# A fused attention and mixture-of-experts kernel on one core: the second group's layer norm is computed ahead of the first unit's products

## Chip, cores and metric

The kernel runs on one core of one Trainium2 chip. The time is that of one execution on the device, in microseconds; three runs of the kernel before are shown. Engines are named as in the profile: PE is TensorE, DVE is VectorE, ACT is ScalarE, POOL is GpSimd, SP is SyncE, whose queue issues most loads and stores.

## What is computed

The input x has 16 batches of 128 channels by 256 positions. There are two stages, each gated and added to x:

```python
# stage 1: k = v = ctx, q = layernorm(x over the 256 positions), 16 heads of 8 channels
kv  = einsum('bhil,bhjl->bijhl', k, v)              # 8 x 8 products of a head
y   = causal convolution of kv with ssm_kernel      # one filter of 256 taps per head
out = einsum('bijhl,bhil->bjhl', y + kv * D, q)
x   = x + tanh(g_xattn) * out
# stage 2: xt = layernorm(x), 2048 tokens of width 256
probs = softmax(xt @ Wg); expert = argmax(probs)     # 8 experts, at most 256 tokens each
routed = gate * (silu(xt @ W1[e]) * (xt @ W3[e])) @ W2[e]
shared = (silu(xt @ sw1) * (xt @ sw3)) @ sw2
x   = x + tanh(g_ffn) * (routed + shared)
```

The layer norm subtracts the mean and divides by the root of the variance plus 1e-5. All arrays are float32.

## The kernel before

**Tiling of stage 1.** The 16 batches are cut into 4 groups of 4. A group's 16 heads are cut into 8 units of 2 heads, so stage 1 has 32 units, 0 to 31, and a unit has one slot of the main loop on each engine (`for s in range(SLOTS)`). The convolution of a head is a product with a Toeplitz matrix (tile `toep`), which the DMA engines read from a padded filter in memory.

- POOL and ACT multiply the context by itself into planes (tile `kv`, a ring of 5 sets of four heads): POOL the mixed products (`kv_products`, lines 433 and 436), ACT the squares (`squares`, line 697). A set serves two units. A set waits for its group's context and for a free place in the ring, that is, for sums of earlier units.
- PE convolves a unit (`convolve`, lines 1055 and 1058) into one of two PSUM tiles `z`. It needs the planes, the Toeplitz rows, and the products of the unit two before, which free its tile.
- DVE multiplies the sums by the queries (`products`, six instructions of line 452) and writes `terms`. It needs `z` and the group's queries `qr`.
- After the 8 units of a group, PE turns the terms back and sums them (`turn_r`, line 1083), and DVE adds them to x (`first_residual`, line 846).

**Queries of a group.** They come out of four steps on four engines. DVE takes the statistics (`norm_stats`, lines 822 to 828: four bn_stats, four bn_aggr, then the variance plus epsilon in `veps` and minus the mean in `mneg`). POOL takes the root by a power and the bias (`scale_and_bias`, lines 578 and 579). ACT applies both (`norm1`, line 676, four batches). PE turns the result (`turn_q`, line 1070), and ACT copies it out of PSUM (`q_copy`, lines 706 and 711). The second group's queries are read first by the products of unit 8.

**What sets the order.** Each engine runs its own list in program order, and semaphores join the lists. Two tables of slots, `STEPS` and `LAST_STEPS`, say at which slot of the loop a step of a group stands; `due(step, s)` gives the group whose step is due at slot s. For the second group (group 1) the statistics stand at slot 1, behind the products of unit 1; the root and the norm at slot 2, behind the planes of that slot; the turning at slot 5. Group 0 is prepared ahead of the loop. The semaphores `stats_done`, `rstd_done` and `xn_done` count the norms in the order of the list `norms`. `norm_stats` also waits until the root before has read `veps` and `mneg`, and `scale_and_bias` until the norm before has been applied.

**Around the first units.** Ahead of the loop DVE adds the skip weight to the diagonal of the first two Toeplitz matrices (line 990). In slot 4, behind the products of unit 4, it copies the router's weights into the shared weight tile (line 1004). POOL makes three constants (lines 594 to 598) between the third set of planes and the loop. The SP queue loads, in this order: x of group 0, the first Toeplitz rows, x of group 1, the filter's store, the rest of the Toeplitz rows with the context of group 1 between, the gates, router and shared weights, x of groups 2 and 3, the context of group 2, and later that of group 3, which waits for the planes of group 1.

**Stage 2** routes the tokens, runs the shared network between and behind the last units, scatters the tokens to memory by expert, and runs the experts one after the other. The change does not touch it.

Of the kernel before, what the change touches and what calls it, by code (L numbers as in the profile page):

```python
# [91 lines left out]
def due(step, s):  # L92

    if step in PREPARING:
        g, late = divmod(s - STEPS[step], UNITS)
        return g + 1 if late == 0 and 0 < g + 1 < NG else -1
    if s == CONV + LAST_STEPS[step]:
        return NG - 1
    g, late = divmod(s - STEPS[step] - UNITS, UNITS)
    return g if late == 0 and 0 <= g < NG - 1 else -1  # L100
# [96 lines left out]
def build(nc, x, ctxt, kpad, skip_d, g_x, g_f, wg, w1, w3, w2, sw1, sw3, sw2, out):  # L197
# [5 lines left out]
    with ExitStack() as ctx:  # L203
# [3 lines left out]
        def sem(name):  # L207
            return ctx.enter_context(nc.semaphore(name))
# [80 lines left out]
        x_in = [sem(f"x_in{g}") for g in range(NG)]  # L289
# [133 lines left out]
        def kv_planes(g, i, o, a, dims_kv, dims_ct):  # L423

            return (view(kv, (4 * g + i) % KVRING * KVQ + o, [[KVH, 4], *dims_kv]),
                    view(ct, (g % 2) * H * CW + 4 * quarter(g, i) * CW + a, [[CW, 4], *dims_ct]))

        def kv_products(eng, g, i, first, done):

            n = 4 - first  # L430
            dst, left = kv_planes(g, i, 64 * first, 0, [[64, n], [1, 64]], [[0, n], [1, 64]])
            _, right = kv_planes(g, i, 0, PL * first, [], [[PL, n], [1, 64]])
            eng.tensor_tensor(dst, left, right, ALU.mult)  # L433
            dst, left = kv_planes(g, i, 256, 0, [[1, 32]], [[1, 32]])
            _, right = kv_planes(g, i, 0, 32, [], [[1, 32]])
            eng.tensor_tensor(dst, left, right, ALU.mult).then_inc(done, 1)
# [128 lines left out]
        def _(pool):  # L565
# [25 lines left out]
            kv_place_free(pool, 0, 1)  # L591
            for c in range(1, 4):
                kv_products(pool, 0, c, 1, kv_pool)
            pool.affine_select(out=tri[:, :], in_=ones[:, :], compare_op=ALU.is_ge, fill=0.0, base=-1,
                               pattern=[[1, P]], channel_multiplier=-1).then_inc(pool_consts, 1)
            pool.iota(ebase[:, :, :], pattern=[[0, GB], [CAP, E]], base=0, channel_multiplier=0,
# [16 lines left out]
            for s in range(SLOTS):  # L613
                g, i = kv_due(s)
                if g >= 0:
                    kv_place_free(pool, g, i)
                    kv_products(pool, g, i, 1, kv_pool)
                if 1 <= s <= CONV and unit(s - 1)[0] >= FULL_TERMS:
                    fold(s - 1)
                for what in ("ln1", "ln2"):  # L620
                    if due(what + "_scale", s) >= 0:
                        scale_and_bias(NORM_AT[(what, due(what + "_scale", s))])
                if s == SLOTS - 1:
                    pool.wait_ge(z_ready, CONV)
                    pool.memset(bg[:, :, :, :], 0.0).then_inc(pool_consts, 1)
                g = due("scatter", s)
                if g >= 0:
                    if g == 0:
                        pool.wait_ge(xd_zeroed, 16 * 4)
                    if g >= 2:  # L630
                        pool.wait_ge(scattered[g % 2], 16 * GB)
                    pool.iota(xrow[:, g % 2, :, L + 1:L + 2], pattern=[[P, GB], [1, 1]], base=1 + g * GB * P,
                              channel_multiplier=1, allow_small_or_imprecise_dtypes=True).then_inc(numbered, 1)
                    pool.wait_ge(numbered, g + 1)
                    pool.wait_ge(dest_done, g + 1)
                    pool.wait_ge(gate_done, g + 1)
                    for b in range(GB * g, GB * (g + 1)):
                        pool.indirect_dma_start(  # L638
                            out=xd, out_offset=bass.IndirectOffsetOnAxis(ap=dest[:, b:b + 1], axis=0),
                            in_=xrow[:, g % 2, b % GB, :], in_offset=None, bounds_check=E * CAP - 1,  # L640
                            oob_is_err=False).then_inc(scattered[g % 2], 16)
                if s == SPLIT_SLOT:
                    split_up()
# [26 lines left out]
        def _(act):  # L670
# [28 lines left out]
            def q_copy(g):  # L699
                o = (g % 2) * H * QPL * PL  # L700
                if g >= 2:
                    act.wait_ge(prods, UNITS * (g - 1))
                for k in range(BLK):
                    n = TP_AT[("q", g, k)]
                    act.wait_ge(tp_ready, n + 1)
                    act.activation(view(qr, o + GB * k, [[QPL * PL, H], [PL, DH], [1, GB]]),
                                   view(tp[n % 2], 0, [[DH, H], [1, DH], [P, GB]]),
                                   ACT.Copy).then_inc(tp_free_act, 1)

                act.wait_ge(tp_free_act, sum(BY_ACT[k[0]] for k in TP[:TP_AT[("q", g, 1)] + 1]))  # L710
                act.activation(view(qr, o + DH * PL, [[QPL * PL, H], [1, 4 * PL]]),
                               view(qr, o, [[QPL * PL, H], [1, 4 * PL]]), ACT.Copy).then_inc(q_done, 1)
# [58 lines left out]
            for c in range(1, 4):  # L771
                squares(0, c)
            q_copy(0)
            for s in range(SLOTS):
                if s == ROUTER_SLOT:
                    act.wait_ge(small_in, 16 * 3)
                    act.activation(tg[:, :], gates[:, :], ACT.Tanh).then_inc(tanh_done, 1)
                if s in SHARED_AT:
                    silu(FU_AT[SHARED_AT[s]])
                if kv_due(s)[0] >= 0:  # L780
                    squares(*kv_due(s))
                if due("ln1_apply", s) >= 0:
                    norm1(due("ln1_apply", s))
                if due("turn_q", s) >= 0:
                    q_copy(due("turn_q", s))
                if due("ln2_apply", s) >= 0:
                    norm2(due("ln2_apply", s))
                if due("turn_xT", s) >= 0:
                    xT_high(due("turn_xT", s))
                if due("exp", s) >= 0:  # L790
                    exponentials(due("exp", s))
                if s == SPLIT_HIGH:
                    weights_high(0)
                if s == EXPERT_SPLIT_SLOT - 1:
                    weights_high(1)
                if s >= XE_SLOT:
                    xe_high(s - XE_SLOT)
# [9 lines left out]
        def _(dve):  # L807
# [181 lines left out]
            for h in range(2):  # L989
                dve.scalar_tensor_tensor(out=toep[:, h, 0:P], in0=anti[:, :], scalar=d_bc[:, h:h + 1],  # L990
                                         in1=toep[:, h, 0:P], op0=ALU.mult, op1=ALU.add).then_inc(diag_added, 1)
            for s in range(SLOTS):
                for k in range(2):
                    if due(f"residual{k}", s) >= 0:
                        first_residual(due(f"residual{k}", s), k)
                    if due("tokens_low", s) >= 0:
                        turned_low(due("tokens_low", s), k)
                if due("ln2_stats", s) >= 0 and s >= CONV:
                    norm_stats(NORM_AT[("ln2", due("ln2_stats", s))])
                if s < CONV:  # L1000
                    products(s)
                if s == ROUTER_SLOT:
                    dve.wait_ge(small_in, 16 * 3)
                    dve.tensor_copy(pads[:, 0:2, 0:E], wg_sb[:, :, :]).then_inc(router_placed, 1)
                if s in SHARED_AT:
                    feed_forward(FU_AT[SHARED_AT[s]])
                if due("ln1_stats", s) >= 0:
                    dve.wait_ge(x_in[due("ln1_stats", s)], 16)
                    norm_stats(NORM_AT[("ln1", due("ln1_stats", s))])
                if due("ln2_stats", s) >= 0 and s < CONV:  # L1010
                    norm_stats(NORM_AT[("ln2", due("ln2_stats", s))])
                if due("logits", s) >= 0:
                    choose(due("logits", s))
                if due("gate", s) >= 0:
                    gate(due("gate", s))
                if due("places", s) >= 0:
                    slot_of_token(due("places", s))
                if s == SPLIT_SLOT:
                    weights_low(0)
                if s == EXPERT_SPLIT_SLOT:  # L1020
                    weights_low(1)
                if s >= XE_SLOT:
                    expert_tokens_low(s - XE_SLOT)
                    tokens_of_slots(s - XE_SLOT)
# [212 lines left out]
```

## Time and profile before

| what | value |
|---|---|
| median of 3 runs | 230.75 us (230.36 to 231.74) |
| time of the profiled execution | 230.07 us |
| its span, first to last instruction | 228.3 us |
| mean granted TensorE clock | 0.989 of full speed |
| PE busy | 197.4 us, 86% |
| DVE busy | 149.6 us, 66% |
| POOL busy | 127.2 us, 56% |
| ACT busy | 80.6 us, 35% |

The span leaves out what lies around the first and the last instruction, so the time of an execution is a little longer. Busy shares are means over stages of different kinds; what a change in the first 35 us is worth has to be read from the waits there. A square bracket at the end of a timeline row gives the engine's idle time before it and what ended that. Neighbouring instructions of one kind are merged in a row (x and their count), and rows can overlap a little, since instructions are pipelined.

### The profile page before, as it was taken

The numbers are of one execution on the slowest core, as the hardware profiler recorded it, in microseconds if no ns is written. First come the engines' busy times: TensorE is split into PE (matmuls) and PEld (weight loads), VectorE is DVE, ScalarE is ACT, GpSimd is POOL, SyncE is SP. The second block draws the span as 40 slices with busy tenths as digits, with TensorE's granted clock in tenths as the row PEclk, the third lists the DMA queues.
The fourth block names the chain that finished last, engine by engine and source line by source line (L and its number), as shares of the span: only waits on it lengthen the run. The fifth ranks groups of instructions, "written<-read, shape, count | busy, mean of one in ns | idle before, by whom it ended". The sixth has DMA issues, their size and how long they took to land.

```text
span 228.3 us, 3954 instructions
## 1 busy us (share of the span) xinstructions
PE 197.4 (86%) x1344; PEld 178.5 (78%) x1344; DVE 149.6 (66%) x483; ACT 80.6 (35%) x153; POOL 127.2 (56%) x129
## 2 busy tenths in 40 slices
PE   0295799977999899899998968997989999999970
PEld 0264679956999798888998958896889999999960
DVE  5749878599788987479863844762457655666230
ACT  2331521535542571222331473631253444234200
POOL 3796946177755489524491207064045667777652
PEclk9999999999999999999999999999999999999995
DMA  3779993000000020020310099995464897522221
GB/s 112 265 216 354 372 409 133 0 0 4 3 3 0 0 93 3 0 93 3 138 46 3 0 305 362 354 357 186 134 185 119 267 292 237 180 79 82 67 80 46
DMA packets 24101, 31.87 MB, mean 140 GB/s; under 512 B 3390, under 2 KB 21574, under 8 KB 24080
## 3 DMA queue, kind: packets, MB, share of 16 engines
q1 hardware_dynamic: 21424, 24.75, 32.6%
q0 software_dynamic: 2304, 6.05, 7.9%
q10 hardware_dynamic: 352, 0.81, 1.0%
q8 instruction: 11, 0.18, 0.3%
q14 instruction: 10, 0.08, 0.1%
HBM read 21.32 MB, written 10.54 MB: 140 GB/s over the span
## 4 chain that ended last, share of the span: by engine, by line
PE 64%; DMA 9%; DVE 9%; issue 5%; ACT 5%; POOL 4%; POOLq 1%; ACTq 0%; SPq 0%; DVEq 0%
PE fb L1144 13%; PE tp L1083 10%; PE z L1144 10%; PE z L1058 9%; PE z L1168 8%; PE z L1055 5%; PE fb L1168 5%; DVE terms L452 3%; DMA kskip_scratch<-kp 3%; DMA toep<-kskip_scratch 2%; DVE stats L822 2%; PE tp L1179 2%; POOL xd_scratch L638 1%; ACT xrow L676 1%; POOL rstd L578 1%
## 5 line engine op out<-in xcount | busy, mean ns | idle before, releaser
L452 DVE TENSOR_TENSOR terms<-z,qr 128x512 f32<-128x512 f32 (+2 forms) x192 | 48.9, 323 | 10.4 <-PE z L1058 10.3
L1058 PE MATMUL z<-kv,toep 128*128 128x288 f32 x128 | 42.4, 414 | 0.0
L433 POOL TENSOR_TENSOR kv<-ct 128x768 f32<-128x768 f32 x15 | 28.1, 1875 | 15.4 <-PE z L1058 14.7
L1144 PE MATMUL fb<-xTh,wh_gu 128*128 128x256 f32 (+1 forms) x104 | 32.4, 311 | 0.7 <-issue 0.7
L1055 PEld LDWEIGHTS z<-kv,toep 128*128 128x128 f32 x128 | 22.6, 194 | 12.1 <-issue 8.1
L1055 PE MATMUL z<-kv,toep 128*128 128x144 f32 x128 | 27.5, 298 | 4.4 <-DVE terms L452 3.6
L653 POOL DMA_INDIRECT kv<-base_scratch,tok x16 | 22.4, 1398 | 15.7 <-DMA base_scratch<-x_sb 11.1
L638 POOL DMA_INDIRECT xd_scratch<-xrow,dest x16 | 17.0, 1065 | 24.8 <-DVE dest L903 21.2
L1144 PE MATMUL fb<-xTl,wh_gu 128*128 128x256 f32 (+1 forms) x104 | 29.0, 279 | 0.0
L1144 PE MATMUL fb<-xTh,wl_gu 128*128 128x256 f32 (+1 forms) x104 | 29.0, 279 | 0.0
L605 POOL TENSOR_TENSOR terms<-terms 128x512 f32<-128x512 f32 x16 | 20.2, 1280 | 11.3 <-DVE terms L452 11.3
L1144 PE MATMUL z<-xTh,wh_gu 128*128 128x256 f32 (+1 forms) x88 | 25.6, 291 | 0.8 <-DVE wl_gu L954 0.8
L1083 PE MATMUL tp<-ident,terms 128*128 128x128 f32 x192 | 23.0, 277 | 1.8 <-DVE terms L452 1.0
L1144 PE MATMUL z<-xTl,wh_gu 128*128 128x256 f32 (+1 forms) x88 | 24.4, 278 | 0.0
L1144 PE MATMUL z<-xTh,wl_gu 128*128 128x256 f32 (+1 forms) x88 | 24.4, 277 | 0.0
L1083 PEld LDWEIGHTS tp<-ident,terms 128*128 128x128 f32 x192 | 22.2, 193 | 2.4 <-DVE terms L452 1.2
L664 POOL DMA_INDIRECT out<-kv,tok x16 | 16.1, 1005 | 12.8 <-DVE kv L930 8.3
L743 ACT ACTIVATE sg<-fb 128x256 f32<-128x256 f32 (+1 forms) x26 | 9.7, 374 | 31.6 <-PE fb L1144 31.6
L1058 PEld LDWEIGHTS z<-kv,toep 128*128 128x128 f32 x128 | 20.5, 195 | 0.0
L1144 PEld LDWEIGHTS fb<-xTh,wh_gu 128*128 128x128 f32 (+1 forms) x104 | 19.3, 185 | 1.6 <-issue 0.9
L1144 PEld LDWEIGHTS fb<-xTh,wl_gu 128*128 128x128 f32 (+1 forms) x104 | 19.3, 185 | 0.8
L1144 PEld LDWEIGHTS fb<-xTl,wh_gu 128*128 128x128 f32 (+1 forms) x104 | 19.3, 186 | 0.0
(121 smaller groups left out, 377.9 us busy)
## 6 DMA issues: line engine op xcount, KB each, us to landing
terms<-w SPq DMA_DIRECT2D x16, 352.0 KB, 4.2
ct<-ctxt SPq DMA_DIRECT2D x3, 768.0 KB, 7.5
xd_scratch<-xrow SPq DMA_DIRECT2D x4, 516.0 KB, 9.5
kv<-xd_scratch SPq DMA_DIRECT2D x8, 258.0 KB, 3.2
out<-x_sb SPq DMA_DIRECT2D x8, 256.0 KB, 2.3
base_scratch<-x_sb SPq DMA_DIRECT2D x8, 256.0 KB, 2.8
terms<-w SPq DMA_DIRECT2D x8, 256.0 KB, 4.7
x_sb<-x SPq DMA_DIRECT2D x3, 512.0 KB, 6.3
```

The costliest lines, as they stand in the source:

```text
L433: eng.tensor_tensor(dst, left, right, ALU.mult)
L452: return eng.tensor_tensor(view(terms, t0 + row * TROW + col, [[64, 2], *td]), view(src, zo, [[512, 2], *zd]), view(qr, q0 + qo, [[CW, 2], ...
L605: pool.tensor_tensor(low, low, high, ALU.add).then_inc(folded, 1)
L638: pool.indirect_dma_start(out=xd, out_offset=bass.IndirectOffsetOnAxis(ap=dest[:, b:b + 1], axis=0), in_=xrow[:, g % 2, b % GB, :], in_off ...
L653: pool.indirect_dma_start(out=bg[:, e % BRING, t, :], out_offset=None, in_=base, in_offset=bass.IndirectOffsetOnAxis(ap=tok[:, e, t:t + 1] ...
L664: pool.indirect_dma_start(out=out_rows, out_offset=bass.IndirectOffsetOnAxis(ap=tok[:, e, t:t + 1], axis=0), in_=fin[:, e % 2, t, :], in_o ...
L743: act.activation(sg[0:n, k % SGS, :], bank[0:n, 0:256], ACT.Silu).then_inc(silu_done, 1)
L1055: pe.matmul(view(z[s % 2], k * 512 + GB, [[PL, NPL], [1, GB]]), toep[:, h, P:2 * P], view(kv, o, [[PL, NPL], [1, GB]]), start=True, stop=F ...
L1058: mm = pe.matmul(z[s % 2][:, k, 0:KVH], toep[:, h, 0:P], view(kv, o, [[1, KVH]]), start=False, stop=True, skip_group_check=True)
L1083: mm = pe.matmul(tp[n % 2][:, j * P:(j + 1) * P], src, ident[:, :], is_transpose=True, start=(t == 0), stop=(t == terms_of(g) - 1))
L1144: mm = pe.matmul(bank[0:rows(blk, c), m * 256:(m + 1) * 256], wt[w % 2][:, col:col + rows(blk, c)], xt[:, place, k, first:first + 256], st ...
L1168: mm = pe.matmul(bank[:, t * L:(t + 1) * L], hidden(blk, c)[0:rows(blk, c), t * P:(t + 1) * P], down[0:rows(blk, c), c * L:(c + 1) * L], s ...
```

## The change

For group 1 alone, three steps leave their slots. The statistics on DVE now stand ahead of the loop, behind the diagonal and ahead of the products of unit 0. The root and bias on POOL stand behind the third set of planes and ahead of the three constants. The norm on ACT stands behind the first group's query copies and ahead of the squares of the first slot. The turning of the queries stays at slot 5, and the other groups' steps stay where they were. No step is added or left out, and no load is moved. Since two lines are inserted above them, line numbers of the changed kernel are one to four higher.

```diff
--- before.py
+++ after.py
@@ -591,6 +591,7 @@
             kv_place_free(pool, 0, 1)
             for c in range(1, 4):
                 kv_products(pool, 0, c, 1, kv_pool)
+            scale_and_bias(1)
             pool.affine_select(out=tri[:, :], in_=ones[:, :], compare_op=ALU.is_ge, fill=0.0, base=-1,
                                pattern=[[1, P]], channel_multiplier=-1).then_inc(pool_consts, 1)
             pool.iota(ebase[:, :, :], pattern=[[0, GB], [CAP, E]], base=0, channel_multiplier=0,
@@ -618,7 +619,7 @@
                 if 1 <= s <= CONV and unit(s - 1)[0] >= FULL_TERMS:
                     fold(s - 1)
                 for what in ("ln1", "ln2"):
-                    if due(what + "_scale", s) >= 0:
+                    if due(what + "_scale", s) >= 0 and (what, due(what + "_scale", s)) != ("ln1", 1):
                         scale_and_bias(NORM_AT[(what, due(what + "_scale", s))])
                 if s == SLOTS - 1:
                     pool.wait_ge(z_ready, CONV)
@@ -771,6 +772,7 @@
             for c in range(1, 4):
                 squares(0, c)
             q_copy(0)
+            norm1(1)
             for s in range(SLOTS):
                 if s == ROUTER_SLOT:
                     act.wait_ge(small_in, 16 * 3)
@@ -779,7 +781,7 @@
                     silu(FU_AT[SHARED_AT[s]])
                 if kv_due(s)[0] >= 0:
                     squares(*kv_due(s))
-                if due("ln1_apply", s) >= 0:
+                if due("ln1_apply", s) >= 2:
                     norm1(due("ln1_apply", s))
                 if due("turn_q", s) >= 0:
                     q_copy(due("turn_q", s))
@@ -989,6 +991,8 @@
             for h in range(2):
                 dve.scalar_tensor_tensor(out=toep[:, h, 0:P], in0=anti[:, :], scalar=d_bc[:, h:h + 1],
                                          in1=toep[:, h, 0:P], op0=ALU.mult, op1=ALU.add).then_inc(diag_added, 1)
+            dve.wait_ge(x_in[1], 16)
+            norm_stats(1)
             for s in range(SLOTS):
                 for k in range(2):
                     if due(f"residual{k}", s) >= 0:
@@ -1004,7 +1008,7 @@
                     dve.tensor_copy(pads[:, 0:2, 0:E], wg_sb[:, :, :]).then_inc(router_placed, 1)
                 if s in SHARED_AT:
                     feed_forward(FU_AT[SHARED_AT[s]])
-                if due("ln1_stats", s) >= 0:
+                if due("ln1_stats", s) >= 2:
                     dve.wait_ge(x_in[due("ln1_stats", s)], 16)
                     norm_stats(NORM_AT[("ln1", due("ln1_stats", s))])
                 if due("ln2_stats", s) >= 0 and s < CONV:
```

On DVE, around the first products, before (`terms` are the products, `stats`, `mv`, `veps` and `mneg` the statistics):

```order
L990 SCALAR_TENSOR_TENSOR toep<-anti,d_bc,toep 128x128 x2
L452 TENSOR_TENSOR terms<-z,qr 128x2x4x64
L452 TENSOR_TENSOR terms<-z,qr 128x128
L452 TENSOR_TENSOR terms<-z,qr 128x2x3x40
L452 TENSOR_TENSOR terms<-z,qr 128x2x24
L452 TENSOR_TENSOR terms<-z,qr 128x2x2x16
L452 TENSOR_TENSOR terms<-z,qr 128x2x2x8
```

The same six products follow once more for unit 1, and then:

```order
L452 TENSOR_TENSOR terms<-z,qr 128x2x2x8
L822 BN_STATS stats<-x_sb 128x6 x4
L825 BN_AGGR mv<-stats 128x2 x4
L827 TENSOR_SCALAR veps<-mv 128x4
L828 TENSOR_SCALAR mneg<-mv 128x4
L452 TENSOR_TENSOR terms<-z,qr 128x2x4x64
```

The same place of DVE in the changed kernel:

```order
L992 SCALAR_TENSOR_TENSOR toep<-anti,d_bc,toep 128x128 x2
L824 BN_STATS stats<-x_sb 128x6 x4
L827 BN_AGGR mv<-stats 128x2 x4
L829 TENSOR_SCALAR veps<-mv 128x4
L830 TENSOR_SCALAR mneg<-mv 128x4
L452 TENSOR_TENSOR terms<-z,qr 128x2x4x64
L452 TENSOR_TENSOR terms<-z,qr 128x128
```

The ten instructions of the statistics moved from behind the products of unit 1 to the place right behind the diagonal; the products of units 1 and 2 are now neighbours.

On POOL, from the third set of planes of group 0 to the third of group 1, the difference (`rstd` is the root, `nbias` the bias, `tri`, `ebase` and `prio` the constants):

```order
 L433 TENSOR_TENSOR kv<-ct 128x4x192
 L436 TENSOR_TENSOR kv<-ct 128x4x32
-L594 AFFINE_SELECT tri<-ones 128x128
-L596 IOTA ebase 128x32
-L598 IOTA prio 128x32
+L578 TENSOR_TENSOR rstd<-veps,mhalf 128x4
+L579 TENSOR_TENSOR nbias<-mneg,rstd 128x4
+L595 AFFINE_SELECT tri<-ones 128x128
+L597 IOTA ebase 128x32
+L599 IOTA prio 128x32
 L433 TENSOR_TENSOR kv<-ct 128x4x192
 L436 TENSOR_TENSOR kv<-ct 128x4x32
 L433 TENSOR_TENSOR kv<-ct 128x4x192
 L436 TENSOR_TENSOR kv<-ct 128x4x32
-L578 TENSOR_TENSOR rstd<-veps,mhalf 128x4
-L579 TENSOR_TENSOR nbias<-mneg,rstd 128x4
 L433 TENSOR_TENSOR kv<-ct 128x4x192
```

Root and bias moved ahead of the constants and of two sets of planes of group 1; the constants themselves stay where they were but for their line numbers.

## Rows read from the trace of the kernel before

**Rows 1.** The page: busy time of each engine, and the ended-last chain by engine.
```profile
PE 197.4 (86%) x1344; PEld 178.5 (78%) x1344; DVE 149.6 (66%) x483; ACT 80.6 (35%) x153; POOL 127.2 (56%) x129
...
PE 64%; DMA 9%; DVE 9%; issue 5%; ACT 5%; POOL 4%; POOLq 1%; ACTq 0%; SPq 0%; DVEq 0%
```

**Rows 2.** The chain of waits in order of time: start us, us, what.
```profile
23.50 0.96 POOL rstd L578
...
26.91 1.09 PE tp L1070 x8
...
34.36 3.57 PE tp L1083 x32
```

**Rows 3.** Timeline of TensorE: start us, us, engine, line, operation, out<-in, [idle before].
```profile
17.32 0.48 PE L1055 MATMUL z<-kv,toep 128*128 128x144 f32 x2 [0.41 <-DMA toep<-kskip_scratch]
...
22.59 0.48 PE L1055 MATMUL z<-kv,toep 128*128 128x144 f32 x2 [2.12 <-DVE terms L452]
...
26.91 1.09 PE L1070 MATMUL tp<-ident,xn 128*128 128x128 f32 x8 [1.16 <-ACT xn L676]
...
31.20 0.48 PE L1055 MATMUL z<-kv,toep 128*128 128x144 f32 x2 [0.27 <-DVE terms L452]
```

**Rows 4.** Timeline of VectorE, 9 to 31 us.
```profile
9.86 2.19 DVE L990 SCALAR_TENSOR_TENSOR toep<-anti,d_bc,toep 128x128 f32<-128x128 f32 x2
15.34 3.15 DVE L452 TENSOR_TENSOR terms<-z,qr 128x512 f32<-128x512 f32 x12 [3.29 <-PE z L1058]
18.41 1.39 DVE L822 BATCH_NORM_STATS2 stats<-x_sb 128x6 f32<-128x256 f32 x4
...
20.25 0.68 DVE L827 TENSOR_SCALAR veps<-mv 128x4 f32<-128x4 f32 x1
...
20.91 2.98 DVE L452 TENSOR_TENSOR terms<-z,qr 128x512 f32<-128x512 f32 x12
24.33 1.54 DVE L452 TENSOR_TENSOR terms<-z,qr 128x512 f32<-128x512 f32 x6 [0.43 <-PE z L1058]
25.79 0.76 DVE L1004 COPY shared_gu<-wg_sb 128x16 f32<-128x16 f32 x1
26.47 1.53 DVE L452 TENSOR_TENSOR terms<-z,qr 128x512 f32<-128x512 f32 x6
```

**Rows 5.** Timeline of POOL, 14 to 27 us.
```profile
14.10 1.80 POOL L433 TENSOR_TENSOR kv<-ct 128x768 f32<-128x768 f32 x1
15.87 0.45 POOL L436 TENSOR_TENSOR kv<-ct 128x128 f32<-128x128 f32 x1
...
16.69 0.16 POOL L598 IOTA prio<- 128x32 f32 x1
19.09 1.81 POOL L433 TENSOR_TENSOR kv<-ct 128x768 f32<-128x768 f32 x1 [2.24 <-PE z L1058]
...
23.46 1.01 POOL L578 TENSOR_TENSOR rstd<-veps,mhalf 128x4 f32<-128x4 f32 x1
...
24.70 1.82 POOL L433 TENSOR_TENSOR kv<-ct 128x768 f32<-128x768 f32 x1
```

**Rows 6.** Timeline of ScalarE, 19 to 27 us.
```profile
19.04 0.72 ACT L697 ACTIVATE kv<-ct 128x256 f32<-128x256 f32 x2 [5.62 <-DMA ct<-ctxt]
24.78 2.07 ACT L676 ACTIVATE xn<-x_sb,nbias,rstd 128x256 f32<-128x256 f32 x4 [5.02 <-POOL nbias L579]
```

**Rows 7.** Loads issued at 2.79, 12.12, 12.67, 22.80: KB, us from issue to landing.
```profile
x_sb<-x SPq DMA_DIRECT2D x1, 512.0 KB, 8.2
...
ct<-ctxt SPq DMA_DIRECT2D x1, 768.0 KB, 6.9
toep<-kskip_scratch SPq DMA_DIRECT2D x1, 512.0 KB, 7.8
...
ct<-ctxt SPq DMA_DIRECT2D x1, 768.0 KB, 7.5
```

## The prediction

> **What bounds the kernel now.** I read the page first: TensorE is busy for 86% of the span and holds 64% of the chain that ended last, VectorE is second with 66% and 9% [rows 1]. So a saving off that chain is worth nothing, and the question is what the chain does around the first units. The chain of waits [rows 2] shows that, from the third unit on, the path leaves TensorE: at 23.50 it lies on POOL, in the root of the second group's variance, and it comes back to TensorE only with the turning of that group's queries at 26.91. The reader should see that the second group's norm is on the path although the queries are first used in unit 8. The timeline of TensorE [rows 3] shows it from the engine's side: it stands still for 2.12 us before unit 4 (22.59), released by VectorE's products, and for 1.16 us before the turning (26.91), released by ScalarE. The timeline of VectorE [rows 4] gives the first wait its cause: products of units 0 and 1 from 15.34 to 18.41, then the statistics from 18.41 to 20.91, and only then the products of unit 2, whose sums were ready at 19.05 (unit 2 starts at 17.32 and a unit that starts after a wait takes 1.73, as 22.59 to 24.33 shows). The same rows show a hole of 3.29 us in VectorE ahead of 15.34. From 34.36 (the first turning back of results) to the end the chain runs through compute; the transfers in it [rows 1] lie in the start and behind the last scatter.
>
> **The change, part by part.** I write U for VectorE's six multiplications of a unit, 1.53 us (18.41 less 15.34, over two), and C for a convolution: the two from 31.20 to 34.36 [rows 2, 3] take 3.16, 1.70 for the one that starts after a wait (1.73 until VectorE is on it) and 1.46 for the one behind another. Between the end of a U and the C that it releases I take 0.15 (U2 ends at 22.44, which is 20.91 + 1.53; C4 starts at 22.59).
>
> *Statistics into the hole.* They are ten instructions, 2.50 us with the hold that one of them met (18.41 to 20.91). VectorE is free at 12.05 (9.86 + 2.19 [rows 4]). The load of x for group 1 is issued at 2.79 and lands 8.2 later, at 11.0 [rows 7], so no wait is added, with 1.05 us in hand. From the first bn_stats to veps it took 1.84 (18.41 to 20.25), which brings 13.9. The next, veps, was held before: 0.68 instead of about 0.17, ending at 20.93 when POOL's multiplication (19.09 + 1.81) ended [rows 4, 5]. Here it would meet POOL's small multiplication and be through by about 14.3; if mneg were held too, by the one that POOL starts at 14.10, it would be 15.90 [rows 5]. U0 starts at 15.34 in the first case and 0.6 later in the second. I take the first, since before, where POOL's next multiplication followed its last at once, mneg met no second hold and the products began at 20.91. The sum below comes out the same either way, which the copy decides.
>
> *Root on POOL.* Now behind its third product set, which ends at 16.32, and ahead of three constants (16.32 to 16.85, 0.5 us). Root and bias took 1.24 (23.46 to 24.70) and end at 17.6, the constants at 18.1; its next work starts at 19.09 on the landing of the second context at 19.0 (12.12 + 6.9 [rows 7]), so this costs nothing, with 0.9 us of cover. What is gained is that POOL goes from its second set of group 1 straight to the third: that one starts at 23.46, where the root stood, instead of 24.70 [rows 5].
>
> *Norm on ScalarE.* 2.07 us from 17.65 to 19.7, in what was an idle stretch of 5.62 us [rows 6]. Two squares that ran at 19.04 move to 19.7 and are needed first by C8. The DMA queue is not moved past anything: its waits (on the first group's planes) are met before it comes to them.
>
> *Convolutions and products.* C2 is unchanged, 17.32 to 19.05, released by its Toeplitz load. U2 19.05 to 20.58, C3 ends 20.51, U3 20.58 to 22.11. C4 starts at 20.73 (its rows of the Toeplitz tile land at 12.67 + 7.8 = 20.5 [rows 7], just in time) and ends 22.46; C5 ends 23.92; U4 22.46 to 23.99. The turning of queries follows C5 at once: 23.92 to 25.02, since the norm is long done; it was 26.91 to 28.00. C6 ends 26.48.
>
> *The copy becomes the late one.* Behind U4 VectorE copies the router's weights. Before, this took 0.76 us for 16 elements, from 25.79 to 26.55, and POOL's multiplication ran from 24.70 to 26.52 [rows 4, 5]: the copy ended when POOL let go. Now the copy is issued at 23.99 while POOL's has run since 23.46 and ends at 25.28. I take it held to there, 1.3 us instead of 0.76, because both rows (this one and veps) end with POOL's instruction and not after a time of their own. By the row's plain duration it would be over at 24.75 and the gain below would be 2.97. The Trainium skill (SBUF — State Buffer, "Who interferes with whom") says that a copy or tensor_scalar in a two-port mode and a GpSimd instruction exclude each other for the whole instruction, whoever is first. By that rule the hold is the full 1.3 us; by a sharing of bandwidth it would be the 0.76. The trace agrees with the rule in the row cited.
>
> *To the sum.* U5 25.23 to 26.76; C7 waits for it, 26.91 to 28.64; U6 26.76 to 28.29; C8 28.64 to 30.10; U7 28.64 to 30.17; C9 30.32 to 32.05. The first turning back of results starts at 32.05, before at 34.36: **2.3 us earlier**. Gone are 2.12 and 1.16 of waiting; new are 0.4 before C7 and 0.2 before C9, with some tenths of slower restarts. VectorE has U8 and U9 behind C8 and C9 as before, so both engines carry the same shift, and POOL rejoins it (its later sets wait for sums). Behind this point I count no loss: the third context lands at 30.3 (22.80 + 7.5 [rows 7]), long ahead of C16 that needs its first planes.
>
> Against the profiled execution (span 228.3, time 230.07, so 1.77 around it): 225.98 + 1.77 = 227.8. The median of the runs shown is 230.75, 0.7 above that execution; I predict for it **228.4**, 1.0% less. What a measurement can tell from no change here is about 1%, 2.3 us, so the forecast lies on that line.
>
> **The rivals.**
> *A, the above*: 228.4, its own range 228.0 to 228.9 (the terms of 0.15 and the restarts may each be off by some tenths). Chance 0.62.
> *B, the copy is not held* or is short enough: gain 3.0 to 3.1, 227.7. For it: each of the two holds is one case. Against: both end with POOL's instruction. 0.15.
> *C, Toeplitz rows decide.* C4 has 0.2 us between landing and need, in a stretch where the DMA engines are full. Landing 1.3 us later puts C4 to C6 that much later; the copy's hold absorbs part of VectorE's share, and the gain falls to about 1.2, which is also what U5 alone moves (26.47 to 25.23): 229.5. 0.12.
> *D, slower: x of group 1 is late.* VectorE now stands in order before U0 with a wait on that load, and POOL, with the root ahead of the second group's planes, waits for VectorE. Before, U4 ended at 25.87; five U from 15.34 on end at 23.0, so the change loses once U0 starts after 18.2, which is a landing after 15.9. One us later than that costs one us: landing at 17 gives 231.9. The row says 11.0, 4.9 us earlier, which speaks against it. 0.05.
> *E, no change*: the gain is given back at a transfer that does not move, such as the last context or the zeroing of the scratch. Against it: behind 34.36 the chain names no transfer from the input side. 230.7. 0.06.
>
> **The numbers.** The range leaves out D, E and the outer parts of B and C: 227.2 to 229.7. One per cent below is 228.44: about half of A (0.33) and B (0.15) are faster by more, 0.48; the rest of A, C and E are within, 0.46; D and a share of accidents 0.06.
>
> **What would show it.** Statistics between 12.05 and 15 on VectorE with U0 still at 15.34; the root on POOL near 16.3; the norm on ScalarE ended before 20; C4 near 20.7 without a wait of 2 us; the turning near 23.9; a copy of about 1.3 us that ends with POOL's third multiplication of the group near 25.3; the first turning back of results near 32.05; and the same distance from there to the end as before, 193.9 us. A copy of 0.2 us means B; C4 released by a DMA means C; a hole on VectorE behind 12.05 that a load ends means D; a distance above 195 means E. I am wrong if the later stages, which I only shift, answer to the new phase between POOL and VectorE with waits of their own.

## The result and the profile after

| | before | changed |
|---|---|---|
| median of 20 runs each | 231.07 us (229.42 to 233.24) | 228.75 us (227.83 to 231.19) |
| profiled execution: time, span | 230.07, 228.3 us | 228.0, 226.2 us |
| PE, DVE, POOL busy | 197.4, 149.6, 127.2 us | 198.4, 150.3, 126.6 us |
| mean granted clock | 0.989 | 0.995 |

The ratio is 0.9908 with a 95% interval from 0.9882 to 0.9934, that is a gain of 1.5 to 2.7 us. The forecast was 228.4 us and a gain of 2.3 us; the medians differ by 2.32 us. Medians here and below are of all runs, while the ratios leave out runs more than 1.5% above the fastest of the same kernel, so that a ratio can differ a little from that of two medians.

The mean granted clock counts the whole span, also its last microseconds, in which TensorE has no work and the clock is at 0.50. In both of these profiles it is 1.00 in every stretch of 2 us from 16 to 222 us, so 0.989 against 0.995 is no gain of the change.

In what follows U*n* is VectorE's products of unit *n* and C*n* TensorE's convolution of it, as in the prediction. The timeline of VectorE answers to [rows 4] (start us, us, engine, line, operation, and in brackets the idle time before):

```profile
9.20 2.19 DVE L992 SCALAR_TENSOR_TENSOR toep<-anti,d_bc,toep 128x128 f32<-128x128 f32 x2
11.31 1.39 DVE L824 BATCH_NORM_STATS2 stats<-x_sb 128x6 f32<-128x256 f32 x4
...
13.15 0.35 DVE L829 TENSOR_SCALAR veps<-mv 128x4 f32<-128x4 f32 x1
13.41 0.16 DVE L830 TENSOR_SCALAR mneg<-mv 128x4 f32<-128x4 f32 x1
14.79 1.55 DVE L452 TENSOR_TENSOR terms<-z,qr 128x512 f32<-128x512 f32 x6 [1.23 <-PE z L1062]
...
22.27 1.55 DVE L452 TENSOR_TENSOR terms<-z,qr 128x512 f32<-128x512 f32 x6 [0.25 <-PE z L1062]
23.73 1.38 DVE L1008 COPY shared_gu<-wg_sb 128x16 f32<-128x16 f32 x1
25.02 2.99 DVE L452 TENSOR_TENSOR terms<-z,qr 128x512 f32<-128x512 f32 x12
```

The statistics lie in the hole (VectorE's idle time ahead of the first products, 3.29 us before), and 1.23 us of it is left. The copy of 16 elements now takes 1.38 us where it took 0.76. The timeline of POOL, which answers to [rows 5], shows the root at its new place and what held the copy:

```profile
13.02 0.45 POOL L436 TENSOR_TENSOR kv<-ct 128x128 f32<-128x128 f32 x1
13.43 1.80 POOL L433 TENSOR_TENSOR kv<-ct 128x768 f32<-128x768 f32 x1
...
15.62 1.00 POOL L578 TENSOR_TENSOR rstd<-veps,mhalf 128x4 f32<-128x4 f32 x1
...
18.86 1.82 POOL L433 TENSOR_TENSOR kv<-ct 128x768 f32<-128x768 f32 x1 [1.44 <-PE z L1062]
...
23.24 1.83 POOL L433 TENSOR_TENSOR kv<-ct 128x768 f32<-128x768 f32 x1
```

The copy was issued into POOL's multiplication of 23.24 and ended at 25.11, when that one had ended (25.07). veps ended at 13.50 behind POOL's small multiplication (13.47), and mneg, right behind it, was not held by the next. ScalarE's norm, behind [rows 6], is now this row:

```profile
16.93 2.08 ACT L677 ACTIVATE xn<-x_sb,nbias,rstd 128x256 f32<-128x256 f32 x4 [4.18 <-POOL nbias L579]
```

The timeline of TensorE answers to [rows 3]:

```profile
20.53 0.48 PE L1059 MATMUL z<-kv,toep 128*128 128x144 f32 x2
...
23.69 1.04 PE L1074 MATMUL tp<-ident,xn 128*128 128x128 f32 x8
...
26.70 0.48 PE L1059 MATMUL z<-kv,toep 128*128 128x144 f32 x2 [0.51 <-DVE terms L452]
...
30.13 0.48 PE L1059 MATMUL z<-kv,toep 128*128 128x144 f32 x2 [0.27 <-DVE terms L452]
...
31.66 3.75 PE L1087 MATMUL tp<-ident,terms 128*128 128x128 f32 x32
```

C4 starts without the wait of 2.12 us, the turning of the queries without that of 1.16, and C7 and C9 have the two small waits that were forecast. The first turning back is shown from 31.66 here and from 31.83 in the chain; before, the chain had it at 34.36 and the timeline at 34.19.

**A measure free of the start.** The first microseconds differ between executions: the filter's store landed at 11.17 in the profile before and at 10.61 in this one. So I also measure from the start of POOL's first set for group 1, which the second context releases, to the first turning back, both by the timelines: 34.19 - 19.09 = 15.10 us before, 31.66 - 18.86 = **12.80 us** after. By this mark the schedule gained 2.30 us; the forecast's sum gave 2.31. The experiments below are read by the same mark, called M. It repeats to 0.01 us in the changed kernel for a reason: the held copy ends with POOL's third multiplication of group 1, which follows POOL's first without a pause, and all that comes behind the copy follows from it.

### The profile page after: what moved, and what is told of

It is laid out like the page before. It is cut to its first block, busy times and chain, and to the rows that moved or that the text cites. A ratio compares the mean times of both kernels' runs of the same rounds, so it can differ in the third digit from the quotient of the medians.

```text
span 226.2 us, 3954 instructions
## 1 busy us (share of the span) xinstructions
PE 198.4 (88%) x1344; PEld 178.9 (79%) x1344; DVE 150.3 (66%) x483; ACT 80.7 (36%) x153; POOL 126.6 (56%) x129
## 4 chain that ended last, share of the span: by engine, by line
PE 66%; DVE 12%; DMA 8%; issue 5%; ACT 3%; POOL 2%; POOLq 1%; ACTq 0%; DVEq 0%; SPq 0%
PE fb L1148 13%; PE z L1148 10%; PE tp L1087 10%; PE z L1062 10%; PE z L1172 8%; PE z L1059 6%; DVE terms L452 5%; PE fb L1172 5%; DMA kskip_scratch<-kp 3%; DMA toep<-kskip_scratch 2%; DVE wl_gu L956 2%; DVE stats L824 2%; PE tp L1183 2%; POOL xd_scratch L639 1%; DMA xd_scratch<-xrow,dest 1%
## 5 line engine op out<-in xcount | busy, mean ns | idle before, releaser
L654 POOL DMA_INDIRECT kv<-base_scratch,tok x16 | 22.4, 1397 | 15.8 <-DMA base_scratch<-x_sb 11.3
L1059 PE MATMUL z<-kv,toep 128*128 128x144 f32 x128 | 28.0, 302 | 2.9 <-DVE terms L452 2.4
L606 POOL TENSOR_TENSOR terms<-terms 128x512 f32<-128x512 f32 x16 | 20.2, 1282 | 11.3 <-DVE terms L452 11.3
```

The source lines that it names most:

```text
L606: pool.tensor_tensor(low, low, high, ALU.add).then_inc(folded, 1)
L654: pool.indirect_dma_start(out=bg[:, e % BRING, t, :], out_offset=None, in_=base, in_offset=bass.IndirectOffsetOnAxis(ap=tok[:, e, t:t + 1] ...
L1059: pe.matmul(view(z[s % 2], k * 512 + GB, [[PL, NPL], [1, GB]]), toep[:, h, P:2 * P], view(kv, o, [[PL, NPL], [1, GB]]), start=True, stop=F ...
```

## Experiments

Ratios are to the kernel before on the same chip, with their 95% intervals. Three groups of four shared a chip each: e1 to e4, e5 to e8, e9 to e12.

**e1, the changed kernel again.**

> The changed kernel itself, on the same chip as the next three, as their common mark. Theory (copy held by POOL): the first turning back of results (PE, line 1087) starts near 31.8 us as in its first profile, 2.3 to 2.5 us ahead of the kernel before; time 0.990 of before. Rival (gain lies in the phase of the transfers at the start, which differed by 0.6 us between the two profiles): that distance changes with the landing of the filter's store, and falls under 2 us when both start alike.

Measured: 229.08 us, ratio 0.9888 (0.9832 to 0.9944). The filter's store landed at 10.9 this time, between the two profiles, and M is 31.67 - 18.87 = 12.80. In e12, the same kernel again, it landed at 11.3, later than in the profile before (11.17), and M is 32.02 - 19.22 = 12.80 once more. The first landing is not the cause of the gain.

**e2, the router's copy behind unit 6.**

```diff
-                if s == ROUTER_SLOT:
+                if s == COPY_SLOT:
                     dve.wait_ge(small_in, 16 * 3)
                     dve.tensor_copy(pads[:, 0:2, 0:E], wg_sb[:, :, :]).then_inc(router_placed, 1)
```

`ROUTER_SLOT` is 4, `COPY_SLOT` 6.

> Changed kernel with the router's copy two slots later on VectorE, behind the products of unit 6, where POOL should be idle (27.7 to 30.2 us). Theory: the copy takes about 0.2 us instead of 1.38 us; U5 starts behind U4 at about 23.8, the 0.51 us wait before C7 and most of the 0.27 us before C9 go; the first turning back starts at 31.0 to 31.2 instead of 31.8, time 0.6 to 0.8 us under the changed kernel (0.987 of before). Rival (the copy only fills time in which VectorE would wait for TensorE anyway): no change against the changed kernel, turning back at 31.8.

Measured: 228.05 us, 0.986 (0.9799 to 0.992). The copy and what follows it, on VectorE:

```profile
28.37 0.18 DVE L1009 COPY shared_gu<-wg_sb 128x16 f32<-128x16 f32 x1
28.47 1.53 DVE L453 TENSOR_TENSOR terms<-z,qr 128x512 f32<-128x512 f32 x6
```

0.18 us instead of 1.38, since POOL's small multiplication (28.07 to 28.52) was just ending and no other followed it. M = 31.68 - 19.72 = 11.96, 0.84 less than in e1. The turning back came at 31.68 and not at 31.0 to 31.2, since the whole start was 0.85 us later in that execution.

**e3, the same move in the kernel before.**

> Kernel before with the same move of the router's copy and nothing else. Theory: the copy was off the path there, since TensorE stood in the turning of the queries (26.91 to 28.00) and U6 waited 1.51 us for sums; so no change, turning back at 34.3, ratio 1.000 +- 0.002. Rival (the copy costs its 0.6 us wherever it stands): 0.6 us faster, 0.997.

Measured: 231.68 us, 1.0009 (0.997 to 1.0048). No gain: the copy was off the path there, as expected. M is 15.43 and not 15.1, because TensorE's clock fell in the profiled execution. The stretches of TensorE in that trace (stretch, us, busy, granted clock, DMA share, GB/s):

```profile
20.00:22.00 2.00, 0.62 (x4) 1.00 1.15 310
22.00:24.00 2.00, 1.29 (x4) 0.66 1.12 371
24.00:26.00 2.00, 2.00 (x8) 0.50 1.08 348
26.00:28.00 2.00, 2.00 (x14) 0.99 1.13 381
```

Behind the standstill of 2.09 us ahead of C4 the clock was at the lower of its two levels (0.50, 1.2 GHz) until about 26. The profile of the kernel before has the same standstill (2.12 us) and 1.00 in these stretches. The drop cost only 0.3 us here, since the turning waits for the norm anyway.

**e4, the statistics alone.**

The edit is that of the change on VectorE, made to the kernel before; root and norm stay where they were.

```diff
+            dve.wait_ge(x_in[1], 16)
+            norm_stats(1)
             for s in range(SLOTS):
...
-                if due("ln1_stats", s) >= 0:
+                if due("ln1_stats", s) >= 2:
```

> Only the statistics on VectorE moved ahead of the first products; root on POOL and norm on ScalarE stand in slot 2 as before. Theory: the 2.12 us wait before C4 goes, but root and norm still stand behind POOL's second set (near 23.3), the norm is applied near 24.5 to 26.6 and the turning of the queries waits for it until about 26.6: TensorE waits there some 2.9 us instead of 1.2, turning back at 34.0, gain under 0.4 us, 0.999 of before. Rival (the statistics between unit 1 and 2 were the cost): gain 2.0 us or more, 0.991, turning back near 32.

Measured: 233.71 us, 1.0076 (1.0035 to 1.0117): slower than before, which neither theory gave. The standstill went where the theory put it, and then something else came. TensorE's row and its stretches:

```profile
26.89 1.56 PE L1072 MATMUL tp<-ident,xn 128*128 128x128 f32 x8 [2.20 <-ACT xn L676]
```

```profile
26.00:28.00 2.00, 1.11 (x7) 0.84 1.14 395
28.00:30.00 2.00, 2.00 (x9) 0.50 0.96 390
30.00:32.00 2.00, 2.00 (x11) 0.80 1.04 415
```

The turning started at 26.89 (26.91 before), so the wait ahead of C4 had only moved ahead of the turning. Behind 2.20 us of standstill the clock was at its lower level just where C6 and C7 are on the path, and M grew to 35.86 - 19.06 = 16.80. Whether the clock is the whole of it is tested in e9. The standstill itself was hardly longer than the one ahead of C4 in the kernel before (2.12 us); it stood in front of other work.

The copy of this run limits what was said of POOL. It ran while POOL computed the root, and was not held:

```profile
23.44 1.01 POOL L578 TENSOR_TENSOR rstd<-veps,mhalf 128x4 f32<-128x4 f32 x1
24.53 0.20 POOL L579 TENSOR_TENSOR nbias<-mneg,rstd 128x4 f32<-128x4 f32 x1
```

```profile
24.23 0.17 DVE L1006 COPY shared_gu<-wg_sb 128x16 f32<-128x16 f32 x1
```

e7 and e9 show the same (0.17 us at 24.37 inside a root from 23.86, 0.16 us at 24.17 inside one from 23.68). So a busy POOL is not enough for the hold; in all the runs that show it, POOL was in a multiplication of planes.

**e5, the norm on ScalarE at its old slot**, statistics and root early.

> Statistics and root early as in the changed kernel, but ScalarE applies the norm in slot 2 as before, behind the squares of slots 0 and 2. Theory: ScalarE is free there and the norm ends by about 21.7, two us before the turning of the queries (23.7), so nothing changes against the changed kernel: turning back near 31.8, 0.990 of before. Rival (each of the three moves carries its part): the norm waits behind the squares for the second context and sums, and 0.5 us or more of the gain is lost.

Measured: 229.24 us, 0.9892 (0.9824 to 0.9961), M = 32.39 - 19.59 = 12.80. The third of the three moves carries nothing.

**e6 and e7, x of group 1 loaded late**, with the changed order and with the old.

```diff
-            load_x(1)
             sp.wait_ge(skip_added, 1)
...
             load_toeplitz(1)
+            load_x(1)
             load_ctx(1)
```

> Changed kernel with the load of x for group 1 issued behind the second part of the Toeplitz rows (about 12 us instead of 2.8), ahead of the second context. Rival D made true: landing near 17.5 to 18 us, VectorE stands in a hole behind the diagonal until then, U0 starts near 20 instead of 14.8, POOL's root waits for the statistics and the second group's planes wait for POOL. Turning back near 36, time 4 us over the changed kernel and 0.5 to 1 us over the kernel with the old order and the same late load. If the theory of the break-even (loss from a landing after 15.9 us) is wrong, it is still the faster of the two.

> Kernel before with the same late load of x for group 1. Units 0 and 1 are multiplied first, so the statistics wait little (landing near 18, needed at 18.4); the second context comes about 1.3 us later and with it POOL's root and the turning. Turning back at 35.5, 1 to 1.3 us slower than before (1.005). If the rival of the transfers at the start is right, it changes as much as the changed kernel does.

Measured: e6 234.23 us, 1.0122 (1.0048 to 1.0196); e7 232.85 us, 1.0025 (0.9982 to 1.0068). With a late load the changed order is the slower one, by 1.4 us in the medians where 0.5 to 1 was expected; the two intervals just overlap. From the trace of e6, VectorE, POOL and the stretches of TensorE:

```profile
17.18 1.41 DVE L824 BATCH_NORM_STATS2 stats<-x_sb 128x6 f32<-128x256 f32 x4 [5.78 <-DMA x_sb<-x]
```

```profile
19.35 1.01 POOL L578 TENSOR_TENSOR rstd<-veps,mhalf 128x4 f32<-128x4 f32 x1 [3.69 <-DVE mneg L830]
```

```profile
18.00:20.00 2.00, 0.00 (x0) 1.00 1.09 365
20.00:22.00 2.00, 1.13 (x4) 0.51 1.16 313
22.00:24.00 2.00, 2.00 (x7) 0.50 1.09 360
```

The load landed at 17.15, 1.25 us behind my break-even of 15.9, and by that rule the loss against the kernel before should have been about 1.3 us. The turning back came at 37.46, 3.3 us later than before, and the medians differ by 2.7. The rule left out the clock, which fell to 0.50 at about 20, within a standstill of 5.35 us, and stayed there until about 27: C2 and C3 took 5.9 us (20.87 to 26.76), where the kernel before needs 3.15 (17.32 to 20.47). The turning back of e7 is at 36.27, not 35.5; its profiled execution was the slowest of the ten (234.72 us), and TensorE stood 2.98 us ahead of the turning with the lower clock behind it (0.50 from 28 to 30), so I take no more from it.

**e8, the copy on ScalarE.**

```diff
+                    act.wait_ge(dve_consts, 5)
+                    act.activation(pads[:, 0:2, 0:E], wg_sb[:, :, :], ACT.Copy).then_inc(router_placed, 1)
...
-                if s == ROUTER_SLOT:
-                    dve.wait_ge(small_in, 16 * 3)
-                    dve.tensor_copy(pads[:, 0:2, 0:E], wg_sb[:, :, :]).then_inc(router_placed, 1)
```

> Changed kernel with the router's copy on ScalarE in slot 4, behind the tanh of the gates, instead of on VectorE. Theory (hold by POOL of a VectorE copy): ScalarE is not held, its copy takes about 0.2 us while POOL multiplies, VectorE goes from U4 to U5 without a pause, and the turning back starts at 31.0 to 31.2: 0.6 to 0.8 us under the changed kernel, the same as with the copy in slot 6. Rival (not the engine pair but the load of the weights holds the copy): ScalarE's copy takes or waits as long as VectorE's did.

Measured: 229.57 us, 0.9889 (0.9844 to 0.9934). ScalarE's copy, and POOL in the same trace:

```profile
22.39 0.20 ACT L783 ACTIVATE shared_gu<-wg_sb 128x16 f32<-128x16 f32 x1
```

```profile
20.95 1.82 POOL L433 TENSOR_TENSOR kv<-ct 128x768 f32<-128x768 f32 x1
```

0.20 us in the midst of a POOL multiplication (20.95 to 22.77): ScalarE is not held. M = 30.66 - 18.77 = 11.89, as in e2.

**e9, the statistics alone, with TensorE kept at work.**

```diff
+                if g == 1:
+                    fill(16)
                 pe.wait_ge(xn_done, g + 1)
```

This is added to the kernel of e4. `fill(n)` issues n transposes of the identity into the free turning bank, where the turning overwrites them.

> Statistics alone moved, as in e4_stats_only, with 16 idle transposes of the identity on TensorE (0.136 us each by the turning's 1.09 us for 8, 2.2 us in all; their result is overwritten) in the wait for the norm. Theory (in e4_stats_only the standstill of 2.2 us ahead of the turning was followed by a granted clock of 0.50, which stretched C6 and C7): the clock stays 1.00 there, the turning starts as before near 26.9, and the turning back comes 15.1 us after POOL's first set of group 1 starts, as in the kernel before, instead of 16.8; ratio 1.000 to 1.002 instead of 1.008. Rival (statistics alone cost by something on VectorE or POOL): 16.8 us stay and the ratio stays 1.008.

Measured: 231.7 us, 0.9981 (0.9942 to 1.002), M = 34.41 - 19.29 = 15.12. The fill and the turning on TensorE, and its stretches:

```profile
23.96 1.91 PE L1068 MATMUL tp<-ident 128*128 128x128 f32 x16
27.13 1.09 PE L1080 MATMUL tp<-ident,xn 128*128 128x128 f32 x8 [1.26 <-ACT xn L676]
```

```profile
26.00:28.00 2.00, 0.87 (x8) 1.00 1.14 371
28.00:30.00 2.00, 2.00 (x14) 1.00 0.98 390
```

The clock stays at 1.00 and all 1.7 us that e4 had lost in M (16.80 less 15.12) are back. So the statistics alone are worth nothing (15.12 against 15.10), and what made e4 slower was the clock.

**e10, the kernel before with both standstills filled.**

> Kernel before with 15 idle transposes ahead of C4 (2.0 us in the standstill of 2.1) and 8 ahead of the turning (1.1 us in the wait of 1.16); results overwritten. Theory (the gain of the change is the schedule's 2.3 us; a low clock behind the early standstill, as one profile of e3_before_copy_slot6 showed, costs 0.3 us at most since the norm is waited for anyway): turning back 15.1 us after POOL's first set of group 1, ratio 0.999 to 1.001, and runs with a low mean clock stay, fewer perhaps. Rival (part of the measured gain of the change is the clock that its shorter standstill keeps): ratio 0.997 or less.

Measured: 231.09 us, 0.9986 (0.9947 to 1.0025), M = 34.08 - 18.96 = 15.12. The schedule gains nothing by the fill. The runs show one thing more. I count the runs whose mean granted clock was below 0.9875: 1 of 12 here, 18 of 29 of the kernel before beside it. So the fill may remove most of these. The ratio gives it 0.1%, and the interval leaves room for 0.5%; over all runs the medians differ by 0.55% (231.09 against 232.37). That is not settled.

**e11 and e12, the copy on ScalarE and the changed kernel, once more.**

> The changed kernel with the router's copy on ScalarE again, for its size: turning back 11.9 us after POOL's first set of group 1, 0.85 us under the changed kernel, ratio 0.985 to 0.988. Rival: the later stages take the 0.85 us back and it equals the changed kernel.

> The changed kernel once more as the mark for the other three: turning back 12.8 us after POOL's first set of group 1, ratio 0.989 to 0.991.

Measured: e11 229.5 us, 0.9881 (0.983 to 0.9933); e12 229.67 us, 0.9864 (0.9823 to 0.9904). e12 has M = 12.80, the fourth profile with this number. e11 has 12.5 and not 11.9: the filter's store landed at 12.0 there, and with the copy off VectorE, POOL's start no longer sets the path. C8 waits for VectorE's products in e11 and for POOL's planes in e2 and e8, so M is the wrong mark for e11. From the turning of the queries to the turning back it takes 32.40 - 25.17 = 7.23 us, as in e8 (30.66 - 23.44 = 7.22), while the changed kernel takes 7.97, 8.14 and 8.11 in its first profile, e1 and e12. So 0.75 to 0.9 us are gained up to this point each time. At the start of the last scatter's transfer they are still seen: it comes 132.47 and 132.48 us behind POOL's first set of group 1 in e2 and e8, and 133.08 to 133.46 behind it in the four profiles with M = 12.80. At the end of the program they are not settled: against the changed kernel on the same chip the medians stand at 228.05 to 229.08 (e2, e1) and 229.5 to 229.67 (e11, e12), but 229.57 to 229.24 (e8, e5).

**A second place of the low clock.** The profile of e12 is 2.2 us longer than the first one of the same program, and its mean granted clock was 0.983. The low level came neither in the start nor in the middle, but behind the last scatter, where TensorE stands until its transfers land (stretches of TensorE):

```profile
158.00:160.00 2.00, 1.51 (x7) 0.78 1.03 360
160.00:162.00 2.00, 2.00 (x6) 0.50 0.06 14
162.00:164.00 2.00, 2.00 (x12) 0.87 0.00 0
```

In the first profile the clock is 1.00 there, and what runs from 158.58 to 166.49 takes 7.91 us; in e12 it takes 9.60 (159.11 to 168.71). So 1.7 us of the difference between two runs of one program lie in a stage that the change does not touch. e3 and e7 have this drop as well as the early one, with mean clocks of 0.975 and 0.976. e4, on the other side, had the early drop alone and a mean of 0.988.

## Why the prediction was right, step by step

*Statistics into the hole*: right. x of group 1 landed at 10.4, 0.9 us ahead of VectorE; U0 waited for sums as before. veps was held for 0.2 us and mneg not, the first of my two cases.

*Root on POOL*: right. 15.62 instead of 16.32 (the whole start was 0.6 to 0.7 us earlier); the constants ended at 17.4, 1.44 us ahead of the next set. The third set of group 1 started at 23.24 (forecast 23.46).

*Norm on ScalarE*: right in its cost and without use. It ended at 19.0, and e5 shows that it could have stayed.

*C4 and the turning*: C4 at 20.53 (20.73), the turning at 23.69 (23.92). Rival C, late Toeplitz rows, did not come: no DMA released C4, which followed C3 (ended at 20.43) here and waited for U2 in e1.

*The copy*: right, and it was the term that decided the size. 1.38 us, ended at 25.11 (25.28). With its old 0.76 the forecast's sum would have given 2.97. e2 and e8 show that it was on the path (M falls by 0.84 and 0.91), that POOL was the holder (0.18 us where POOL's multiplication was at its end, 0.20 on ScalarE in the midst of one), and e3 that it was free before the change. In six profiles the copy ended 0.02 to 0.04 us behind POOL's large multiplication, to which it was held for 0.76 to 1.40 us. The prediction took any POOL instruction to hold the copy for its whole length; the root did not (e4), which changes nothing here, since the copy meets a multiplication. Rival B is what these two kernels are: with the copy not held, the gain up to the turning back was 3.1 and 3.2 us (15.10 less 11.96 and 11.89), where B had 3.0 to 3.1.

*The sum*: 2.30 us by M in the first profile, e1, e5 and e12, against 2.31. C7 waited 0.51 instead of 0.4 and C9 0.27 instead of 0.2, and both started some 0.2 early with the second context, which landed that much sooner. One wait is new and was not forecast: POOL's first set of group 2 now waits 2.52 us for the third context and starts at 30.20, 0.9 earlier than before where all else is 2.1 to 2.5 earlier. It costs nothing that these runs show; POOL's next set starts 2.1 earlier (32.40 against 34.50).

*The distance to the end*, which I had left unchanged at 193.9 us, was 226.2 - 31.83 = 194.4. Two things make this up. Some 0.1 to 0.4 us are lost ahead of the last scatter: from the first turning back (by the chain) to the transfer of the scatter it takes 120.02 and 119.97 us in the profiles of the kernel before and of e10, and 120.20, 120.34 and 120.12 in the three of the changed kernel. But e9, which gained nothing in M, has 120.18, so whether the change costs them stays open. The rest lies in the transfers behind the scatter, which differ between executions of one kernel. Before, in the changed kernel's first profile, and in e1:

```profile
154.38 2.85 DMA xd_scratch<-xrow,dest
157.30 2.69 DMA kv<-xd_scratch
```

```profile
152.03 3.07 DMA xd_scratch<-xrow,dest
155.16 2.66 DMA kv<-xd_scratch
```

```profile
152.18 3.80 DMA xd_scratch<-xrow,dest
156.04 2.87 DMA kv<-xd_scratch
```

e1 is 0.9 us longer in these two rows than the first profile of the same program.

*Rival D* was right in its sign and its place (e6, e7), and too small: each piece of it was priced at full clock. The same omission made my expectation of e4 wrong (0.999 expected, 1.0076 measured). In the forecast it did no harm that the profiles show, because the change shortens TensorE's standstills instead of moving one in front of work on the path.

*How near the number came* is partly luck. The schedule's 2.3 us are shown by M. The runs of the changed kernel spread over 3.4 us, and medians of 20 runs that differ by 2.32 could have differed by 1.5 to 2.7. How much of the median's gain comes from the clock stays open. Over all runs, a mean clock below 0.9875 was seen in 41 of 75 of the kernel before (three chips) and in 12 of 38 of the changed one. That points to some effect, but the mean clock is a poor witness: it also falls by the drop behind the last scatter (e12), and e4's early drop leaves it at 0.988. Among the runs above 0.9875 the medians are 230.95 and 229.07 (e1), 230.62 and 229.25 (e5), 231.24 and 228.62 (e12): 1.4 to 2.6 us, around the schedule's 2.3.

## What to carry to other kernels

When a step is taken off the path, follow each engine's list to the next thing that can be late, down to a copy of 16 elements: here it took back 0.8 of 3.1 us, and the short duration it shows in a profile can be a hold whose length depends on when the other engine's instruction started. A chain over several engines (statistics, root, norm) has to be moved as a whole up to its last late member: the statistics alone gave nothing, statistics and root gave all, the norm's place did not matter. And a waiting time that is only moved can be dearer than before: 2.2 us of standstill in front of work on the path cost 1.7 us through the clock (e4), 2.1 us in front of work that had slack 0.3 (e3).

## What the runs showed of the hardware

- A VectorE copy of 16 elements a partition was held to the end of a running POOL multiplication of planes: 1.38, 1.37, 1.37 and 1.40 us (changed kernel, e1, e12, e5), 0.76 (before) and 0.78 (e10). It took 0.17 us where POOL was idle (e6), and 0.16 to 0.17 inside POOL's root of 1.01 us (e4, e7, e9), which did not hold it. ScalarE's copy was not held by a multiplication either (0.20 us, e8).
- TensorE's granted clock fell to 0.50 within or just behind standstills of 2.09 us (e3), 2.20 (e4), 2.98 (e7) and 5.35 (e6) in the start, and of 1.93 (e12), 2.06 (e7) and 2.73 (e3) behind the last scatter. It did not fall behind 2.12 in the start (before), nor behind 2.27 (e10) and 2.62 (e1) at the scatter. So at one place of one program it falls in some executions and not in others. At the low level convolutions took up to twice as long, and M grew by 1.7 us in e4; the late drop of e12 cost 1.7 us.
- With x of group 1 out of its way, the filter's small store landed 4.4 and 4.9 us after its issue (4.83 to 9.21 in e6, 4.57 to 9.44 in e7) instead of 6.1 to 7.5 in the twelve other profiles. A large load that nobody waits for yet held up the one that opens the path; an order of loads that uses this was not tried.
